# One unread 384-column product ahead of each pair of 8-row score units, in three attention loops

## The reference

```
x = x + tanh(g_xattn[0]) * attention_0(layernorm(x), ctx, ctx, adj, mask)
x = x + tanh(g_ffn[0])   * fp8_linear(layernorm(x))
x = x + tanh(g_xattn[1]) * attention_1(layernorm(x), ctx, ctx, bias, padding)
x = x + tanh(g_ffn[1])   * two rounds of 8 routed experts and a shared one
x = x + tanh(g_xattn[2]) * attention_2(layernorm(x), ctx, ctx, bias, padding)
x = x + tanh(g_ffn[2])   * silu(x @ Wg.T) * (x @ Wu.T) @ Wd.T
x = x + tanh(g_xattn[3]) * latent attention, 8 heads of 64
x = x + tanh(g_ffn[3])   * mixture of 8 experts
```

```
scores  = q @ k.T / sqrt(8) + bias        # q, k: 256 x 8 for each of 4 x 16 (sequence, head)
weights = softmax(where(masked, -inf, scores))
out     = (weights @ v) @ Wo.T + bo
```

## Time and profile before

| | us |
|---|---|
| median of three runs | 791.53 |
| their range | 787.36 to 792.10 |
| the profiled execution's own time | 789.41 |
| its span, first to last instruction | 787.6 |
| TensorE busy in it | 718.6 (91%) |
| VectorE busy | 548.5 (70%) |
| ScalarE busy | 490.2 (62%) |

### The profile page before, as it was taken

How to read it: one execution, slowest core, us unless ns; L and a number is a source line. 1 busy time by engine, 2 the same in 40 slices (tenths; PEclk the granted TensorE clock), 3 DMA queues, 4 the chain that set the end, 5 groups by cost and what they waited for, 6 DMA issues and landing times. The chain is left out here.

```text
span 787.6 us, 15151 instructions
## 1 busy us (share of the span) xinstructions
PE 718.6 (91%) x5098; PEld 403.8 (51%) x5098; DVE 548.5 (70%) x1750; ACT 490.2 (62%) x1343; POOL 171.4 (22%) x163
## 2 busy tenths in 40 slices
PE   6989898899999988998799999988989999899887
PEld 3656664666666322333256666653346666553222
DVE  7699988679997378488858999754065666545533
ACT  3788883578884767698669889416675655422101
POOL 7510321560111177256633000201000000000000
PEclk9899999989999969999899999999999999999889
DMA  5794000274000000000007200000000000000000
GB/s 210 138 294 183 2 2 1 62 143 100 2 2 2 0 1 0 1 0 1 1 1 142 41 2 2 28 1 0 1 1 2 1 1 1 2 0 1 1 1 27
DMA packets 17357, 27.61 MB, mean 35 GB/s; under 512 B 1408, under 2 KB 15360, under 8 KB 16640
## 3 DMA queue, kind: packets, MB, share of 16 engines
q1 hardware_dynamic: 17280, 26.64, 12.7%
HBM read 19.03 MB, written 7.60 MB: 34 GB/s over the span
## 5 line engine op out<-in xcount | busy, mean ns | idle before, releaser
L917 ACT ACTIVATE RING<-RING,NMX 128x256 f32<-128x256 f32 x384 | 191.0, 501 | 37.0 <-DVE NMX L1922 36.9
L1922 DVE CUSTOM_DVE_ANT_0 RING<-bank,ADJM 128x256 f32<-128x256 f32 x384 | 143.9, 414 | 20.6 <-PE bank L1306 18.2
L1353 PE MATMUL bank<-W,RING 128*128 128x128 f32 x768 | 118.5, 280 | 14.1 <-ACT RING L929 12.7
L1353 PEld LDWEIGHTS bank<-W,RING 128*128 128x128 f32 x768 | 88.8, 143 | 35.7 <-ACT RING L917 27.4
L1934 DVE COPY RING<-bank 128x512 f32<-128x512 f32 x144 | 98.6, 686 | 4.1 <-PE bank L1353 3.6
L565 POOL TENSOR_TENSOR small<-small 128x2 f32<-128x2 f32 (+2 forms) x17 | 19.4, 1142 | 254.9 <-DVE small L1783 254.9
L917 ACT ACTIVATION_READ_ACCUMULATOR RING<-RING,NMX 128x1 f32 x384 | 72.9, 190 | 0.0
L831 ACT ACTIVATE RING<-bank,NMX 128x512 f32<-128x512 f32 x64 | 43.3, 683 | 42.4 <-DVE NMX L1851 22.7
L1371 PE MATMUL bank<-RING,ARENA 128*32 128x256 f32 x768 | 62.4, 400 | 0.2
L1511 PE MATMUL bank<-ARENA,W 64*128 64x512 f32 x180 | 60.1, 675 | 2.3 <-DVE ARENA L2140 1.9
L1851 DVE TENSOR_REDUCE NMX<-bank 128x1 f32<-128x512 f32 x64 | 39.4, 678 | 31.9 <-PE bank L1204 31.9
(11 more groups left out here) (272 smaller groups left out, 1322.8 us busy)
## 6 DMA issues: line engine op xcount, KB each, us to landing
scratch<-ARENA SPq DMA_DIRECT2D x18, 192.0 KB, 3.0
ARENA<-scratch SPq DMA_DIRECT2D x6, 576.0 KB, 8.2
W<-in_weights SPq DMA_DIRECT2D x1, 2564.0 KB, 22.2
scratch<-ARENA SPq DMA_DIRECT2D x18, 128.0 KB, 2.7
ARENA<-scratch SPq DMA_DIRECT2D x6, 384.0 KB, 5.8
W<-in_weights SPq DMA_DIRECT2D x2, 1024.0 KB, 13.4
W<-in_weights SPq DMA_DIRECT2D x1, 1905.5 KB, 14.6
scratch<-ARENA SPq DMA_DIRECT2D x18, 64.0 KB, 8.1
```

Of the source, the lines that this page charges most:

```text
L917: nc.scalar.activation(P_OF(n)[:, q * S:(q + 1) * S], S_OF(n)[:, q, :], ACT.Exp, bias=NMX[:, 2 * t + q:2 * t + q + 1], scale=-1.0, accum_o ...
L1353: mm = nc.tensor.transpose(bk[:, o:o + P], P_OF(n)[:, i:i + P], ident)
L1922: nc.vector.tensor_tensor_reduce(out=S_OF(n)[:, q, :], in0=SBANK(n)[:, q * S:(q + 1) * S], in1=ADJM[:, b, q, :], scale=-1.0, scalar=BIG, o ...
```

## The change

One call of `rehearse` is put between the wait for `s_max` and the score products of a pair. It writes 384 columns into the bank that the first unit of the pair is about to write; the score products are issued behind it on the same engine and overwrite it. There are 8 pairs in each of 3 loops, so 24 products, 48 matmul instructions and as many weight loads are added. Nothing is removed, and no wait is added or taken away.

More of the change, by code:

```diff
@@ L1302, in attention @@
                             pe.wait_ge(s_max, 2 * n - 2)
+                        rehearse(1, SBANK(n))
                         for q in range(2):
```

## The result

| | before | changed |
|---|---|---|
| median of four runs, us | 789.58 | 802.95 |
| range | 787.36 to 792.10 | 802.23 to 805.56 |
| span of the profiled execution | 787.6 | 801.0 |

The changed kernel is slower: ratio 1.0178, 95% interval 1.0149 to 1.0208, 13.4 us between the medians and 13.4 us between the profiled spans. The forecast was 799.5 us. The four runs before are the three of the prediction and one more, 787.63 us.

What follows compares the result with a forecast made beforehand. TensorE was taken to bound the float32 parts of the three loops. On the profiled 789.41 us, 15.5 us of added products minus 6.2 us of regained clock gave 798.7, plus 0.7 for an average run 799.5 us; range 793 to 807.

Steps and rivals of the forecast that it cites:

- The direction and the mechanism: Float32 parts of the three loops: TensorE's added time lies on the path one to one, making the kernel slower, 799.5 us.
- What comes back: Float32 parts of loops 1 and 2: the four stretches at half clock go, giving back 6.2 us at most, all expected.
- The 0.7 us that the forecast added for an average run: Whole kernel: the mean of four times, 790.1 us, lay 0.7 above the profiled execution, so 798.7 became 799.5 us.
- the size of the cost: All three loops: 24 added products at 0.645 us each, 15.5 us, with bounds of 13.1 and 17.8 us.
- The sentence behind it: Wait for `s_max` ahead of the pairs: the product cannot fill it, with only 0.2 us to fill in loop 3.
- That the clock still falls: Rival, float32 parts: nothing comes back and products in low stretches cost twice, 807.5 us; 803 with half the falls; chance 0.17.
- That part of the cost is hidden: Rival, float32 parts: some busy time is really short waits, so 0.4 us a product, 793 us; chance 0.15.
- the faster case: Rival, score pairs: TensorE has slack around VectorE's round trip; below 0.26 us per product, 783.2 us at zero; chance 0.05.
- within 1%: Whole kernel: change too small to tell from none, about 7.9 us; chance 0.37, against 0.59 slower and 0.04 faster.

## Why the prediction came out as it did

**The direction and the mechanism were right.** TensorE's time in the parts is on the path one to one. The change adds 6.30 us to loop 3, and 6.4 us (4.3 to 9.9) is what the kernel with loop 3 alone loses; a second product adds 5.16 us a loop; the rest of each loop did not move. VectorE's waits rose to 11.6 us where about 10 was expected.

**What comes back was right for this comparison.** 6.2 us were expected. Against the full-clock parts (25.95, 22.70 and 22.70 us) the changed parts are 6.16, 6.29 and 6.30 us longer, 18.75 in all, and the kernel before's were 3.01, 3.05 and 0 us longer, 6.1 in all. 18.8 - 6.1 = 12.7 us. The 0.7 us that the forecast added for an average run matches the 0.7 us by which the profile grew outside the parts, but that is luck: they have nothing to do with each other. The full clock of loop 2 at 22.70 us is a number for the sum only: the versions with few products show that without added time its part ends at 24.3 to 25.9 us, at the DMA. A kernel that kept the clock without added time would not have given back all of loop 2's 3.05 us.

**The step that failed is the size of the cost**, "24 x 0.645 = 15.5 us", with 17.8 as its upper bound. It measured 18.8 us, 0.78 per product. The streaming was right, as the doubled product shows. Three things stand beside it. At every one of the eight places it is 0.1 us more to the 8-row scores behind it than to another full product; their weights load only when the scores start, which is the likely reason but was not varied. At six of the eight its own first instruction takes 0.07 to 0.11 us longer, after a wait or after products in smaller tiles. And the change of shape that the product takes away, for which the prediction used 0.645 and not 0.74 us at every place, saves only 0.09 us at the two places where four transposes precede it; ahead of steps 8 and 12 TensorE waits that time out. 5.16 + 0.8 + 0.5 - 0.2 = 6.3 us.

**The sentence behind it that failed** is that the product cannot fill the wait for `s_max` because "there is next to none to fill". I had read 0.2 us of waiting in loop 3 and laid the 1.16 us of eight transposes to a change of tile shape. It was mostly a wait: with the product ahead of it they take 0.93 us. The trace models a matmul as busy beyond the moment at which the next can start, so a wait of 0.2 us behind a matmul does not appear as idle time. Issued ahead of the wait, the cost is 5.22 us a loop, which is what I had summed.

**The rivals.** That the clock still falls did not happen; the kernel with 8 rows, whose four runs took 809.68 to 826.65 us, shows what that can cost, more than the 807.5 us I gave it. That part of the cost is hidden did not happen. For the faster case the cost would have had to be below 0.26 us per product; at all 24 places even 128 columns cost about 0.35. The 0.37 that I gave to "within 1%" rested on a sum right at that bound; with the 3.3 us that the cost lacked it lies clearly beyond.

**Falls without gaps.** The Trainium skill, "TensorE: Matmul & The Clock Gate", section "HAM oscillation — how this bites in real kernels", lays falls to long idle gaps between matmuls. The traces show a fall behind a gap of 1.61 us, in the version with three products, though one such case does not show that the gap caused it. They also show falls without such a gap: in the kernel before, where the engine was busy 3.35 of the 3.42 us ahead of one, and in the kernel with 8 rows 27 us at 0.50 in an engine that is busy throughout with 8-row products, transposes and full products among them. With 384 columns in all rows at the same places no part fell. Here the rows of the array in use mattered.

## What to carry to other kernels

Where TensorE sets the pace, as here, a product that holds the clock costs its full streaming time (0.645 us) plus what stands around it (0.14 us more); weigh it against the measured cost of the falls (here 3.0 us for two stretches of 3.4 us) before adding it everywhere. Put it ahead of a wait, not behind one; that was worth 1.1 us a loop here, and three products a loop instead of eight brought the kernel level with the one before. And before counting a stretch's full-clock time as a gain, look for what comes ready next, such as a DMA round trip that the slow stretch had been hiding.

## What the runs showed of the hardware that was not expected

- A small full-array product (128 columns) or one in 8 rows ahead of each pair was followed, in the profile of the slowest run of each, by longer stretches at 0.50 (17.1 and 27.3 us) than no product at all in three profiles (10.2 us at most in a loop). Other runs of the two were faster by up to 13 and 17 us. Why the clock stays down longer there is not settled.
- Eight transposes that show as busy for 1.09 us take 0.93 us of the engine's time when nothing waits.
- Four transposes take 0.58 us ahead of 8-row scores and 0.49 us ahead of a full-array product.
